# Expert biases by transfer, row data on GpSimd, reordered last norms, and the causal mask added on VectorE, in a two-layer decoder kernel

## The reference

```python
def attn(x_q, x_kv, causal):
    Q, K, V = ...                       # 16 heads of 16 columns
    scores = einsum('bqhd,bkhd->bhqk', Q, K) / 4
    if causal: scores = where(tril, scores, -inf)
    return einsum('bhqk,bkhd->bqhd', softmax(scores), V) @ wo + bo

def moe(x):
    topw, topi = top_k(softmax(x @ rw + rb), 2); topw = softmax(topw)
    h = gelu(einsum('td,edf->etf', x, w1) + b1[:, None, :])
    eo = einsum('etf,efd->etd', h, w2) + b2[:, None, :]
    return einsum('etd,te->td', eo, combine(topw, topi))
# layer 1 ends with layernorm(x + moe(x), ln3_g, ln3_b)
```

## Time and profile before

| | |
|---|---|
| median of 3 runs | 1278.37 us (1276.76 to 1280.55) |
| the profiled execution: its own time | 1274.6 us |
| its span, first to last instruction | 1272.8 us |
| busy: PE / DVE / ACT / POOL | 1107.4 / 836.6 / 685.6 / 561.3 us |
| causal calls, c = 0 | about 27 to 201 us of the span |
| causal calls, c = 2 (maxima) | about 443 to 650 us |
| expert tiles | about 918 to 1226 us |
| last norms (first moments to the end) | 1240.8 to 1272.8 us |

### The profile page before, as it was taken

How to read it: one execution, slowest core, us unless ns; L and a number is a source line. 1 busy time by engine, 2 the same in 40 slices (tenths; PEclk the granted TensorE clock), 3 DMA queues, 4 the chain that set the end, 5 groups by cost and what they waited for, 6 DMA issues and landing times. The chain is left out here.

```text
span 1272.8 us, 26559 instructions
## 1 busy us (share of the span) xinstructions
PE 1107.4 (87%) x9056; PEld 911.7 (72%) x9056; DVE 836.6 (66%) x1782; ACT 685.6 (54%) x1445; POOL 561.3 (44%) x805
## 2 busy tenths in 40 slices
PE   8789999999999999999999998877289999989840
PEld 7567677778877888877777666544289998989840
DVE  2666667775555444355676777642479999999945
ACT  4355555665555554445566655644176666656522
POOL 4355555322221113345674554433436565656544
PEclk9899999999999999999999989977589999999985
DMA  7666657573333233446575754405477676767663
GB/s 162 99 134 125 95 81 97 85 126 59 51 49 49 39 36 51 84 59 93 119 104 74 106 91 81 77 26 184 148 231 221 195 226 195 236 192 223 208 159 114
DMA packets 106707, 152.20 MB, mean 120 GB/s; under 512 B 19440, under 2 KB 91376, under 8 KB 99824
## 3 DMA queue, kind: packets, MB, share of 16 engines
q1 hardware_dynamic: 98112, 140.09, 50.5%
q0 software_dynamic: 8352, 10.80, 4.4%
q10 hardware_dynamic: 144, 0.02, 0.0%
HBM read 78.39 MB, written 21.62 MB: 79 GB/s over the span
## 5 line engine op out<-in xcount | busy, mean ns | idle before, releaser
L862 ACT ACTIVATE probs<-s 128x384 f32<-128x384 f32 (+1 forms) x512 | 267.8, 541 | 195.2 <-PE s L680 181.8
L932 DVE TENSOR_REDUCE neg_max<-s 128x2 f32<-128x512 f32 x256 | 169.6, 689 | 95.4 <-PE s L657 89.2
L930 DVE TENSOR_REDUCE neg_blocks<-s 128x3 f32<-128x384 f32 x256 | 135.9, 556 | 120.2 <-PE s L654 112.8
L680 PE MATMUL s<-q_stack,k_stack 98*128 98x256 bf16 (+1 forms) x1024 | 175.6, 262 | 14.4 <-ACT probs L862 11.9
L545 POOL TENSOR_SCALAR_AFFINE_SELECT probs<-probs 128x256 f32<-128x256 f32 x256 | 103.1, 411 | 188.1 <-ACT probs L862 187.0
L1284 PE MATMUL moe<-rows_hi,e_w_hi 128*128 128x256 f32 x368 | 106.1, 288 | 25.1 <-DVE rows_lo L1395 25.1
L680 PEld LDWEIGHTS s<-q_stack,k_stack 98*128 98x128 bf16 x1024 | 90.1, 99 | 41.4 <-ACT probs L862 24.4
L699 PE MATMUL pv<-probs,v 128*32 128x256 f32 (+1 forms) x2048 | 115.2, 367 | 2.7 <-POOL probs L545 2.3
L1399 DVE TENSOR_TENSOR e_hidden_lo<-e_hidden,e_hidden_hi 128x512 fp32r<-128x512 f32 x92 | 108.0, 1173 | 10.7 <-ACT e_hidden_hi L1353 10.7
L657 PE MATMUL s<-k_stack,q_stack 96*128 96x256 bf16 x512 | 98.1, 276 | 12.8 <-DVE neg_max L932 11.2
L1284 PE MATMUL moe<-e_w_hi,e_hidden_hi 128*128 128x256 f32 x368 | 104.6, 284 | 1.6 <-DVE e_w_lo L1391 1.6
(11 more groups left out here) (197 smaller groups left out, 2588.9 us busy)
## 6 DMA issues: line engine op xcount, KB each, us to landing
w<-in_expert_w SPq DMA_DIRECT2D x26, 1024.0 KB, 5.4
k_stack<-k_part SPq DMA_DIRECT2D x192, 128.0 KB, 4.1
q_stack<-q_part SPq DMA_DIRECT2D x192, 128.0 KB, 5.8
e_w<-in_expert_w SPq DMA_DIRECT2D x24, 1024.0 KB, 5.3
rows<-slots_x SPq DMA_DIRECT2D x25, 256.0 KB, 2.9
slots_x<-filler SPq DMA_DIRECT2D x8, 518.0 KB, 3.8
cT<-in_context SPq DMA_DIRECT2D x16, 256.0 KB, 4.8
e_b<-in_expert_b SPq DMA_DIRECT2D x24, 128.0 KB, 3.9
```

The lines of the kernel that those rows point to most:

```text
L680: last = pe.matmul(dst[:, kt * S:kt * S + S - q0], k[:, kt * P:(kt + 1) * P], q[:, q0:S], start=True, stop=True)
L862: act.activation(probs[hd][:, 0:width], s2[hd % 2][:, 0:width], ACT.Exp, scale=SCALE).then_inc(probs_ready, 1)
L930: dve.tensor_reduce(neg_blocks[:, :, hd], src[:, 0:3 * P].rearrange("p (b s) -> p b s", b=3), AX_X, ALU.max, negate=True).then_inc(s1_free, 1)
L932: dve.tensor_reduce(neg_max[:, :, hd], src[:].rearrange("p (t s) -> p t s", t=TILES), AX_X, ALU.max, negate=True).then_inc(s1_free, 1)
```

## The change

1. **Causal mask.** PE no longer multiplies the mask in. DVE adds it, and takes the maximum in the same operation, twice per head: once over the 256 columns of the second query tile and once over the 128 of the first. The sums are written back to the PSUM bank. The copy and the minimum after the 16th head are gone.
2. **Expert bias b1** comes by a transfer of SP, issued after the tile's gelu, in place of `fetch_bias` on DVE.
3. **Row data** (tokens and shares) is computed by POOL after `second_high`, with one operation more; DVE only adds b2.
4. **Last norms.** DVE takes the moments of pair after pair, with each offset one pair behind; then come the shifts, in place in `z`. The gain of tiles 3 and 6 is multiplied by DVE. Gain and shift are loaded at the end of the expert part.

```diff
@@ scores_for_max
-                    pe.matmul(dst[:, P:3 * P], ident_b[:], mask_qk[:].rearrange("p b s -> p (b s)"), start=True, stop=False)
-                    pe.matmul(dst[:, 0:S], q[:, P:S], k, start=False, stop=True, skip_group_check=True)
-                    last = pe.matmul(dst[:, S:S + P], q[:, 0:P], k[:, 0:P], start=False, stop=True)
+                    pe.matmul(dst[:, 0:S], q[:, P:S], k, start=True, stop=True)
+                    last = pe.matmul(dst[:, S:S + P], q[:, 0:P], k[:, 0:P], start=True, stop=True)
@@ row_max
-                    dve.tensor_reduce(neg_blocks[:, :, hd], src[:, 0:3 * P].rearrange("p (b s) -> p b s", b=3), AX_X, ALU.max, negate=True).then_inc(s1_free, 1)
+                    dve.tensor_tensor_reduce(src[:, 0:S], src[:, 0:S], mask_qk[:].rearrange("p b s -> p (b s)"), -1.0, -MASKED, ALU.add, ALU.min, neg_max[:, 1, hd:hd + 1])
+                    dve.tensor_tensor_reduce(src[:, S:S + P], src[:, S:S + P], mask_qk[:, 1, :], -1.0, -MASKED, ALU.add, ALU.min, neg_max[:, 0, hd:hd + 1]).then_inc(s1_free, 1)
...
-                    if CAUSAL[c]:
-                        dve.tensor_copy(neg_max[:, 0, :], neg_blocks[:, 2, :])
-                        dve.tensor_tensor(neg_max[:, 1, :], neg_blocks[:, 0, :], neg_blocks[:, 1, :], ALU.min)
-                        dve.drain()
@@ moe_part, sync: step
                 sp.wait_ge(row_data_ready, n + 1)
                 fetch_about(at, i)
+
+                sp.wait_ge(hidden_ready, (n + 1) * QUARTERS)
+                fetch_first_bias(e, i)
@@ moe_part, gpsimd
+            def row_data(i, nth):
+                pool.wait_ge(about_loaded[i], 16 * nth)
+                pool.wait_ge(b1_loaded[i], 16 * nth)
+                pool.wait_ge(added[i], ADDED * nth)
+                pool.sem_inc(gate, 1)
+                pool.tensor_copy(token[i][:], about[i][:, :, 0].bitcast(U32))
+                pool.tensor_scalar(chosen[i][:], about[i][:, :, 1], b1_e[i][:, FC:FC + 1], 1.0, ALU.is_equal, ALU.subtract)
+                pool.tensor_scalar(less[i][:], about[i][:, :, 2], 2.0, 1.0, ALU.mult, ALU.subtract)
+                pool.drain()
+                pool.tensor_tensor(chosen[i][:], chosen[i][:], less[i][:], ALU.mult)
+                pool.drain()
+                pool.tensor_tensor(share[i][:], chosen[i][:], about[i][:, :, 2], ALU.add).then_inc(row_data_ready, 1)
...
                     second_high(i, j + 1)
+                    row_data(i, j + 2 - i)
                     add_rows(n - 1, 1 - i, j + 2 - i)
@@ moe_part, vector
-                    fetch_bias(n + 1, 1 - i)
...
-                    row_data(i, j + 2 - i, j + 2 - i)
                     add_bias(n - 1, 1 - i, j + 1)
...
+            dve.wait_ge(norm_loaded, 16 * 2)
             for pair in range(B // 2):
...
+                variances(pair)
+                if pair > 0:
+                    offset_of(pair - 1)
+            shift_of(0)
+            offset_of(B // 2 - 1)
+            for b in range(1, B):
                 shift_of(b)
```

123 lines of the change are left out of this document (58 added, 65 removed).

## The result

The changed kernel takes 1295.4 us (median of 4 runs, 1293.5 to 1298.7) where the kernel before takes 1279.0 in the same runs: ratio 1.016, interval 1.0121 to 1.0198. It is slower, where I forecast 41 us less; its time lies above the range. Its profiled execution took 1293.45 us, with a span of 1291.6; that of before 1272.8.

| stretch | before, us | after, us | difference | forecast |
|---|---|---|---|---|
| start to the last addition to x | 897.7 | 888.6 | -9.2 | -22 |
| from there to the first moments | 343.1 | 379.1 | +36.1 | -10 |
| first moments to the end | 32.0 | 24.0 | -8.1 | -8 |

A forecast was written before the change was run, and what follows sets the result against it. PE was busiest (1107.4 of 1272.8 us), but the edits touch stretches with different limits. Attention 22, row data and bias 10 and last norms 8 take 40 us off 1274.6: 1234.6, forecast 1238 us from 1278.4, range 1226 to 1270.

The forecast's parts named there:

- The mask on PE and DVE: Attention: PE saves 1.78 us a causal call, DVE's head takes 0.69 us; 8, 7 and 7 us, together 22.
- The estimate of 0.77: DVE's new causal head in us, priced from the skill page's cycle costs; would give about 1248 us.
- PE's full 1.78: Causal calls of c = 2: all of PE's saving of 1.78 us a call comes, 7 us in four calls.
- Row data off DVE: Expert tiles: 0.70 us leaves the loop through DVE's result; 0.45 us a tile taken, 10 us in 22 tiles.
- idle 4.06 us: Expert tile: POOL's wait for DVE's result, said to hold its five tiny operations, about 1.4 us with drains.
- The sum's section on new waits: Expert part: POOL's casts and transfers queue behind its wait for the b1 transfer, issued a tile before; ACT waits too.
- w1 chain: SP's expert queue: one more transfer, some 0.65 us, against ACT's slack of 1.10; leaves 0.57 us a tile.
- The bias copy: Expert tile on DVE: copy and register load hidden by ACT's gelus, so removing them saves nothing.
- C: Rival: the expert part gives nothing, as small operations hold DVE's low parts or w1 lands late; 1248 us, chance 0.16.
- B: Rival: slower, DVE bounds the causal calls; at 1.03 us a head 11 us lost, 1289 us; chance 0.12.
- the signs that I said would prove me wrong: Calls over 22.4 us with PE idle before a head's first matmul; ACT's w1 wait before PE's; POOL late for the result.
- The last norms: End of kernel: first moments to last shift falls from 29.3 to 21.5 us; 8 us gained, bounds 5 and 11.

The follow-up runs named there:

- short_max: Kernel before with the mask edit alone, DVE's second maximum of a causal head taken over 16 of its 128 columns: 1255.7 us, ratio 0.9818.
- rows_behind: Changed kernel with the row data back on DVE, made behind the result instead of ahead of it: 1262.9 us, ratio 0.9896.
- behind_late: rows_behind with late_about's order on SP: 1254.8 us, ratio 0.9808.
- rows_on_dve: Changed kernel with the row data back on DVE ahead of the result, b1 still by a transfer: 1252.4 us, ratio 0.9797.
- late_about: Changed kernel with only SP's order altered: what the next tile's row data and b1 need is fetched behind w1: 1248.8 us, ratio 0.9784.
- w1_behind: late_about with SP holding w1 back until POOL has issued the scatter of the tile before: 1422.1 us, ratio 1.1161.
- warm_mask: Kernel before with the mask edit alone, plus one idle PE transpose a head in the first two calls: 1269.6 us, ratio 0.9945.

## Why the prediction was right or wrong

**The mask on PE and DVE.** Right in the main for c = 0: about half of what PE saves comes back as time. DVE's head takes part in the limit, though it is not alone (short_max). The head was priced at 0.69 us and measures 0.63. The estimate of 0.77 from the Trainium skill (VectorE: DVE Perf Modes, the section on the TRN2 errata) is further off; the trace speaks against it here as it did for the reduction of 384 columns. A call of c = 0 gains 0.8 us for the 0.9 to 1.0 forecast. The term was over-sized elsewhere. In c = 2 I let PE's full 1.78 come, since DVE's waits exceeded what PE could give; 0.5 to 1.1 came, PE waits for DVE's maxima there too (3.4 us in 9 waits), and short_max shows that a shorter head still helps. The waits counted over a stretch are not all usable in the place where the maxima stand. The start, which I left out, is longer: the first call ends at 89.7 to 93.5 us in the kernels with the new maxima, at 86.6 to 88.4 in the three with the old. Together 9.2 us (11 to 12 alone) for 22.

**Row data off DVE.** This is the step that failed, and with it the sign. I followed the loop result, POOL, cast, low part, and took 0.70 us out of it. I wrote that POOL's five operations "lie in its idle 4.06 us". They lie there in length, but not in what they wait for. On DVE the row data waited too, for the scatter of two tiles before; they were never seen waiting, because they came late: those of the earlier trace rows start 7.3 us after the second transfer's issue, and so do all the others from the third tile on. On POOL they come right behind the cast, before the scatter has landed, and the scale and the next scatter stand behind that wait. The sum's section on new waits named the b1 transfer and not this one, although the wait is in the diff. The runs showed in its place a loop on POOL of landing, row data, scale and scatter, 8.2 and 6.7 us, that sets the tile at 14.8 us; with the row data back on DVE the 43 us are gone. The gain itself, 0.45 us a tile for taking 0.70 out of DVE's loop, was found in no kernel: rows_behind and behind_late, made for it, are slower than rows_on_dve.

**SP's queue.** I counted the extra transfer in the w1 chain (0.65 us, of a slack of 1.10) and missed the larger thing: SP waits for the row data before it fetches the next `about`, and w1 is behind it. With the row data 3 to 4 us later, relative to w2, w1 is too. late_about, where only this order differs, gives back 46.6 us. By the chains it does so through the landing: POOL's loop bounds both kernels, w1 issued just behind the scatter goes with a longer landing, and a longer landing with later row data. I had also read only the last wait of ACT as its slack. Before the change it stood 3.2 us a tile for w1 and then 1.10 for PE (24.4 us in 21 waits); now it is 5.5 for w1, and the waits for PE are down to 6.1 us in 8: the slack is used up.

How much of the landing's 2.5 us is w1's place stays open, but the traces say more than "the later w1, the longer". Take the tiles of 17 kernels, from the third tile on (all but w1_behind, warm_mask and short_max), and sort them by w1's issue against the second transfer's. The landing takes 4.3 us on the mean with w1 2 to 3 us ahead (11 tiles), 5.3 with 1 to 2 ahead (36), 6.1 with less than 1 ahead (111), 7.9 with less than 1 behind (102), 6.7 with 1 to 2 behind (42) and 4.7 with 2 to 3 behind (11, all of rows_behind). So it is longest with w1 just behind the scatter and short on either side. w1_behind, with w2 in that place, fits. That w1 is the cause is not shown: no run moved it and nothing else.

**The bias copy.** Priced at nothing, it was worth some 0.4 us a tile: rows_on_dve, with the row data as before, runs 12.5 us a tile for 12.92. In the earlier trace rows DVE had waited only 0.21 us for ACT, and I took that for proof that the copy was hidden.

**Rivals.** C had the right place and the wrong end, 0 as the worst case of the expert part. w1 does come late, as C says, but it is 1% of the changed kernel's chain; the scatter's landing, 12% of it, is in none of the rivals. I bounded the term at nothing from below; in this kernel a new wait in two in-order queues had no such floor. B did not come. Of the signs that I said would prove me wrong, two are in the trace: a w1 wait on ACT ahead of PE's, and POOL late for the result. The first was a poor sign, since the kernel before has that wait in 22 tiles too.

**The last norms** were right in size, 21.2 us for 21.5, by some luck: the last offset comes 1.4 us later than summed, and the shifts and gains behind it take 1.8 less.

## What to carry to other kernels

When a step moves to another engine, write down every semaphore that it waits for, and look when each is raised, measured from the new place; a wait that never showed before may only have been covered by the old engine's lateness. Then do the same for who waits for the step: here a transfer of 1 MB stood in an in-order queue behind a wait for four numbers a row. Order such a queue so that nothing urgent stands behind a wait for something slow, and look what the large transfer runs beside at its new time; late_about's few moved lines turn a loss of 1.6% into a gain of 2.2%. And when an experiment gives the rival's number, look at the chain before calling the theory dead: a loop can be there in both kernels and only have become shorter.
